# Gate stage of a graph and expert network: one activation per hidden chunk, its two parts made on VectorE, turned parts evicted by ScalarE, router sums two steps later

## What is computed

```python
x = x + gnn(layernorm(x), src, dst, edge_weight, ...)        # x: 12500 x 256
xf = layernorm(x)
H = gelu(xf @ W1 + b1)                                        # 1024 hidden values per token
probs = softmax(H @ Wg + bg)                                  # 8 experts
assign = argmax(probs)
y = H @ Wd[assign] + bd[assign]
x = x + probs[assign] * y
```

## Time and profile before

| what | us |
|---|---|
| median of 3 runs | 3556.47 (3550.64 to 3558.81) |
| the profiled execution | 3553.28 |
| its span on the core | 3551.5 |
| TensorE matmul busy / VectorE busy / ScalarE busy in the span | 2995.6 / 2470.9 / 1287.2 |
| first matmul of the gate stage's products to the last | 2443.3 to 3075.1 |

### The profile page before, as it was taken

One profiled execution on the slowest core, in us unless ns is written; L12 is line 12 of the kernel. 1 busy time (PEld: TensorE's weight loads), 2 busy tenths in 40 slices (PEclk: granted clock), 3 DMA queues, 4 the chain that ended last, 5 costly groups with the idle time before them and its releaser, 6 DMA issues. The chain is left out here.

```text
span 3551.5 us, 67236 instructions
## 1 busy us (share of the span) xinstructions
PE 2995.6 (84%) x20000; PEld 2455.1 (69%) x20001; DVE 2470.9 (70%) x6086; ACT 1287.2 (36%) x2250; POOL 722.6 (20%) x706
## 2 busy tenths in 40 slices
PE   4776668888888886999999999996888888669998
PEld 2333347777777776888888888444666667469998
DVE  8999557777777774666666666335787777576665
ACT  3111346666666662000000000363545545353332
POOL 1000005555655552000000000000212121212222
PEclk9888559999999998999999999998999999879999
DMA  4221017777777777998999887001334333366664
GB/s 122 81 73 44 1 37 290 282 285 293 294 284 278 287 278 269 318 315 317 316 314 316 316 315 267 6 0 36 138 125 161 137 149 133 122 229 208 211 211 146
DMA packets 214801, 710.45 MB, mean 200 GB/s; under 512 B 28495, under 2 KB 104313, under 8 KB 189514
## 3 DMA queue, kind: packets, MB, share of 16 engines
q1 hardware_dynamic: 130778, 405.55, 34.8%
q0 software_dynamic: 83952, 304.02, 21.8%
HBM read 383.91 MB, written 340.05 MB: 204 GB/s over the span
## 5 line engine op out<-in xcount | busy, mean ns | idle before, releaser
L1232 PE MATMUL coll_ps_sum<-coll_rows,coll_hot 128*128 128x256 f32 x3724 | 822.5, 380 | 19.0 <-DVE coll_hot L1174 18.9
L1232 PEld LDWEIGHTS coll_ps_sum<-coll_rows,coll_hot 128*128 128x128 f32 x3724 | 701.4, 190 | 111.3 <-DVE coll_hot L1174 19.1
L1174 DVE TENSOR_SCALAR coll_hot<-coll_nodes,coll_rows 128x128 f32<-128x128 f32 x1862 | 495.0, 342 | 281.4 <-PE coll_ps_sum L1232 259.6
L927 PE MATMUL send_ps_msg<-send_parts,send_pick 128*128 128x256 f32 x3584 | 547.0, 302 | 25.9 <-ACT send_msg L960 23.6
L801 POOL DMA_INDIRECT messages<-send_msg,send_to x448 | 477.5, 1066 | 383.6 <-ACT send_msg L960 232.7
L960 ACT ACTIVATE send_msg<-send_ps_msg 128x1024 f32<-128x1024 f32 x448 | 456.8, 1026 | 262.5 <-PE send_ps_msg L927 200.0
L927 PEld LDWEIGHTS send_ps_msg<-send_parts,send_pick 128*128 128x128 f32 x3584 | 480.0, 201 | 33.5 <-ACT send_msg L960 26.0
L844 DVE TENSOR_SCALAR send_pick<-send_ps_local,edges_down 128x1024 fp32r<-128x1024 f32 x224 | 287.5, 1284 | 178.3 <-PE send_ps_local L914 86.3
L1265 ACT ACTIVATE nodes_hid<-coll_ps_turned 128x256 f32 (+1 forms) x98 | 37.6, 383 | 810.0 <-PE coll_ps_turned L1078 810.0
L2148 PE MATMUL exp_ps_y<-exp_w_hi,exp_hT_hi 128*128 x840 | 247.0, 294 | 0.9 <-DVE exp_hT_lo L2100 0.9
L1647 ACT ACTIVATE gate_act_h<-gate_ps_h,gate_b_sb 128x512 f32<-128x512 f32 x200 | 137.2, 686 | 294.4 <-PE gate_ps_h L1875 293.3
(11 more groups left out here) (302 smaller groups left out, 5148.4 us busy)
## 6 DMA issues: line engine op xcount, KB each, us to landing
coll_rows<-messages SPq DMA_DIRECT2D x98, 1300.0 KB, 6.7
coll_rows<-messages SPq DMA_DIRECT2D x98, 1170.0 KB, 6.9
exp_pay<-regions SPq DMA_DIRECT2D x105, 646.0 KB
send_window<-node_rows SPq DMA_DIRECT2D x112, 128.0 KB
node_rows<-sort_xn SPq DMA_DIRECT2D x25, 512.0 KB, 5.1
coll_own<-node_rows SPq DMA_DIRECT2D x98, 128.0 KB, 4.3
sort_xt<-in_x_dram SPq DMA_DIRECT2D x24, 512.0 KB, 4.4
gate_xt<-in_x_dram SPq DMA_DIRECT2D x24, 384.0 KB
```

The source lines that it names most:

```text
L927: ins = pe.matmul(ps_msg[:, q % 2, a, :], pick[:, q * RUN + a, :], parts[:, s % 2, part, :], start=(part == 0), stop=(part == 1))
L1174: ins = dve.tensor_scalar(hot[:, j, :], nodes[:], rows[:, s, j, ROW_ID:ROW_ID + 1], rows[:, s, j, ROW_W:ROW_W + 1], ALU.is_equal, ALU.mult)
L1232: ins = pe.matmul(ps_sum[:, s, 0:D], hot[:, j, :], rows[:, s, j, 0:D], start=(j == 0), stop=(j == CJ - 1))
```

## The change

ScalarE applies Gelu once per step, into `act_h`. VectorE rounds `act_h` to `act_hi` with a copy, waits for it, and subtracts. `keep_back` moves from VectorE to ScalarE, behind the Gelu of its step. TensorE adds a step's logits two steps later instead of one, between the two halves of a product; those of step 7 stay where they were, those of step 6 go into the next chunk's first product. GpSimd waits for the payload's evictions itself before it sends.

```diff
@@ -1588,6 +1588,7 @@
                 def send(i, s):
                     pool.wait_ge(where_ready, i + 1)
                     pool.wait_ge(x2_copied, i + 1)
+                    pool.wait_ge(back_ready, KC * (i + 1))
                     pool.sem_inc(pool_turn, 1)
                     for j in range(CH):
                         pool.indirect_dma_start(
@@ -1630,6 +1631,15 @@
                     act.activation(xnT_hi[:, s], ps_x[:].rearrange("p c f -> p (c f)").rearrange("p (k n) -> p k n", k=DH),
                                    ACT.Copy).then_inc(xnT_hi_ready, 1)
 
+                def keep_back(i, s, k, before):
+
+                    if k == 0 and later(i, 2):
+
+                        act.wait_ge(sent[s], 16 * CH * before)
+                    act.wait_ge(back_done, KC * i + k + 1)
+                    act.sem_inc(act_turn, 1)
+                    act.activation(pay[:, s, :, k * P:(k + 1) * P], ps_b[:, k % 2, :, :], ACT.Copy).then_inc(back_ready, 1)
+
                 def keep_logits(i):
                     act.wait_ge(logit_sum, i + 1)
                     if later(i):
@@ -1644,8 +1654,11 @@
                         act.wait_ge(h_done, KC * i + k + 1)
 
                         act.sem_inc(act_turn, 1)
-                        act.activation(act_h[:, k % 2, :], ps_h[:, k % 2, :], ACT.Gelu, bias=b_sb[:, k:k + 1])
-                        act.activation(act_hi[:, k % 2, :], ps_h[:, k % 2, :], ACT.Gelu, bias=b_sb[:, k:k + 1]).then_inc(h_ready, 1)
+                        act.activation(act_h[:, k % 2, :], ps_h[:, k % 2, :], ACT.Gelu, bias=b_sb[:, k:k + 1]).then_inc(h_ready, 1)
+                        if k > 0:
+                            keep_back(i, s, k - 1, before)
+                        elif later(i):
+                            keep_back(i - 1, 1 - s, KC - 1, None)
                         if k == 0 and later(i):
                             keep_logits(i - 1)
                         if k == XN_AT and not is_last(i):
@@ -1654,6 +1667,7 @@
                 second_output(0)
                 keep_xnT(0, 0)
                 all_chunks(act, chunk)
+                keep_back(LAST, 0, KC - 1, None)
                 keep_logits(LAST)
 
             @block.vector
@@ -1711,16 +1725,9 @@
 
                     dve.wait_ge(h_ready, KC * i + k + 1)
                     dve.sem_inc(dve_turn, 1)
+                    steps.link(dve.tensor_copy(act_hi[:, k % 2, :], act_h[:, k % 2, :]))
                     dve.tensor_tensor(act_lo[:, k % 2, :], act_h[:, k % 2, :], act_hi[:, k % 2, :].bitcast(F32),
                                       ALU.subtract).then_inc(act_lo_ready, 1)
-
-                def keep_back(i, s, k, before):
-
-                    if k == 0 and later(i, 2):
-
-                        dve.wait_ge(sent[s], 16 * CH * before)
-                    dve.wait_ge(back_done, KC * i + k + 1)
-                    dve.tensor_copy(pay[:, s, :, k * P:(k + 1) * P], ps_b[:, k % 2, :, :]).then_inc(back_ready, 1)
 
                 def choose(i, s):
 
@@ -1760,10 +1767,6 @@
                 def chunk(i, s, before):
                     steps.restart()
                     for k in range(KC):
-                        if k > 0:
-                            keep_back(i, s, k - 1, before)
-                        elif later(i):
-                            keep_back(i - 1, 1 - s, KC - 1, None)
                         keep_rest(i, k)
                         if not is_last(i):
                             if k == RESIDUAL_AT:
@@ -1787,7 +1790,6 @@
                 keep_xnT_rest(0, 0)
                 all_chunks(dve, chunk)
                 steps.restart()
-                keep_back(LAST, 0, KC - 1, None)
                 choose(LAST, 0)
                 find_places(LAST, 0)
 
@@ -1871,6 +1873,10 @@
                             pe.wait_ge(h_ready, KC * i + k - 1)
 
                         for q in range(DH):
+                            if q > 0 and k >= 2:
+                                add_logits(i, k - 2)
+                            elif q > 0 and k == 0 and later(i):
+                                add_logits(i - 1, KC - 2)
                             for w, a in ((w_hi, xnT_hi), (w_hi, xnT_lo), (w_lo, xnT_hi)):
                                 ins = pe.matmul(ps_h[:, k % 2, :], w[:, q, k * P:(k + 1) * P], a[:, s, q, :],
                                                 start=(q == 0 and w is w_hi and a is xnT_hi),
@@ -1886,9 +1892,7 @@
                             count(i - 1)
                         if k == XN_AT and not is_last(i):
                             turn_xn(i + 1)
-                        if k > 0:
-                            add_logits(i, k - 1)
-                        elif later(i):
+                        if k == 0 and later(i):
                             add_logits(i - 1, KC - 1)
                         if k == 0 and not is_last(i):
                             turn_back(i + 1)
@@ -1897,6 +1901,7 @@
                 turn_xn(0)
                 all_chunks(pe, chunk)
                 back(LAST, KC - 1)
+                add_logits(LAST, KC - 2)
                 add_logits(LAST, KC - 1)
                 turn_logits(LAST)
                 count(LAST)
```

## The result

The changed kernel took 3574.27 us (median of 7 runs, 3553.29 to 3578.45), the kernel before 3556.03 (7 runs): ratio 1.0049, 95% interval 1.003 to 1.0068. The forecast was 3543.3 with a range to 3562, so both the direction and the range were missed.

What follows compares the result with a forecast made beforehand. The prediction took the loop of TensorE, Gelu and VectorE's chain to the normalisation as the bound. 24 x 0.42 plus 3.1 from the clock gave 13.2 us less, 3556.47 to 3543.3, range 3532 to 3562.

Steps and rivals of the forecast that it cites:

- What bounds the kernel: Gate stage: the loop of TensorE, Gelu and VectorE's chain of some 10 us to the normalisation sets the chunk's period.
- Rival B: Gate stage: TensorE becomes the bound, 25 x 2.46 = 60 us less, 3496; chance 0.04.
- The activation and the copy: Step 2: second activation goes, VectorE's copy with link takes 0.46, so the moments start 0.12 us earlier.
- the bounds 0.35 and 0.73: VectorE's copy with link: lower and upper limits around 0.46, for a loop gain of 0.75 or -0.39 us.
- T0: End of the product of step 0 on TensorE's timeline of a full-clock chunk, 2725.41 in the profile before.
- The eviction goes, the copy with its link comes: 0.61 - 0.46 = 0.15 gained in each: VectorE at steps 3 and 4: replacing the eviction by the copy gains 0.15 us in each step.
- The 0.12 of step 2: VectorE at step 2: moments start at 2734.15 and not 2734.27, 0.12 us gained.
- I take it that the falls go, and all of the 3.1 is gained: TensorE's clock: waits of 1.6 and 1.7 bring no falls, saving 0.26 us a chunk, 12 times: 3.1.
- Rival A: TensorE's clock falls behind the second wait in 12 of 24 chunks: 17.9 less 13.2, 4.7 us slower, 3561; chance 0.16.
- a gain of 13.2: Whole gate stage: 24 chunks x 0.42 plus 3.1 from the clock, 13.2 us gained in all.
- The eviction on ScalarE: ScalarE, in the second activation's slot of 0.68: costs nothing, with bounds of 0.57 to 0.69 for its length.
- rival C: Loop shortened less, by bubbles of 0.1 in five places of the loop or falls that stay: 3550 to 3560; chance 0.20.

Runs made afterwards that it cites:

- the last experiment: Changed kernel with the gap before step 3's copy closed, find_places moved behind the normalisation, and GpSimd's x-row copy put before its sends: ratio to the kernel before 0.9887.
- both gaps closed: Changed kernel with VectorE's wait for Gelu and its increment issued before waiting for its last small operation, at steps 3 and 4: ratio to the kernel before 0.9956.
- logits alone: Kernel before with only the logits moved two steps later, inside the next product: ratio to the kernel before 1.0010.
- gap of step 4 closed: Changed kernel with the wait for Gelu and its increment issued early at step 4 only: ratio to the kernel before 0.9975.

## Why the prediction was wrong

**What bounds the kernel** was right: VectorE's row from the moments to the normalisation sets the chunk (closing its gaps shortened the chunk by 0.37, and taking the places out of it by another 1.2 once nothing else was late), the wait for `act_lo` is split and not removed (1.62 and 1.88, forecast 1.6 and 1.7), and the last experiment gains what the shorter row promises. Rival B fell with it.

**The activation and the copy** were right in size: copy 0.43, subtraction 0.46 behind it, as forecast; the bounds 0.35 and 0.73 were not needed. The product of step 2 ended 6.63 after T0 and not 6.54, but T0 came 7.36 behind `turn_xn` and not 7.45 (2705.61 to 2712.97), so TensorE's part of the loop is the 13.99 of the forecast.

**"The eviction goes, the copy with its link comes: 0.61 - 0.46 = 0.15 gained in each"** is the first step that failed. I compared lengths, and took it that the copy would start where the eviction had started. The eviction had been the cover of the wait and increment of `keep_rest`; without it they stood bare, 0.18 at step 3 and 0.18 at step 4 by the kernel with both gaps closed, 0.37 of its interval. The 0.12 of step 2 came, and as much was lost behind it: from the moments to the normalisation 7.95 (2721.79 to 2729.74; 7.82 before, 7.52 forecast), and from the product of step 2 to `turn_xn` 11.56 (2719.60 to 2731.16), where it was 11.57 before (2731.95 to 2743.52) and 11.15 was forecast. So the loop gained nothing. At full clock the interval even went from 25.47 to 25.56, which goes with the delay of the logits, for logits alone has 25.58 with the old row; it is as short as the average before, 25.59 (2472.05 to 3035.03 in 22 intervals), only because the old falls were gone. The prediction itself named gaps in VectorE's chain as a sign that it would be wrong.

**"I take it that the falls go, and all of the 3.1 is gained"** is the second, and the dear one. It rested on a second wait of 1.7, which the gap at step 4 made 1.88. At 1.7 there are indeed no falls (both gaps closed, gap of step 4 closed); at 1.88 there were nine, and they cost 1.6 each, since no wait follows. So the second error came out of the first. Rival A described what happened and its price was near, 1.49 against 1.6, but it had a chance of 0.16. Its sum was made with a gain of 13.2 that was not there: with nearly no gain (22 x 0.03 = 0.7), nine falls of 1.6 are 14.4 - 0.7 = 13.7 slower, against 12.5 measured; the two intervals at the start of the stage gained the 1.1 between them.

**The eviction on ScalarE** cost nothing, as forecast: 0.59, in the slot of the second activation.

```profile
L1641 ACT ACTIVATE gate_pay<-gate_ps_b 128x512 f32<-128x512 f32 x200 | 118.2, 591 | 0.6 <-PE gate_ps_b L1828 0.3
```

**Bubbles inside products**, rival C, are not there: three matmuls, two for the logits and three more took 0.23 each. **GpSimd's new wait** cost nothing: its sends still wait for the places alone, 508.2 us in 25 times and 502.3 before.

The Trainium skill says that a semaphore costs nothing extra between chained VectorE operations (VectorE: DVE Perf Modes, § The DRAIN you can't avoid). Here that holds nearly: the subtraction starts 0.03 behind the end of the copy that it is linked to. But a second wait, on a computed value and with an increment behind it, cost 0.18 more where no long operation ran beside it.

## What to carry to other kernels

Ask of an instruction that is taken away what ran beside it: the sequencer's own work (computing a wait's value, waiting, incrementing) was hidden behind an eviction of 0.69 and cost 0.18 behind an operation of 0.16, and it could be hidden again by putting it between that operation and the wait for it. If a wait of TensorE is split, look at what follows the last part: a fall of the clock that another wait swallows cost 0.2 to 0.3 here, the same fall at the end of the loop 1.6. And moving work off the row that bounds the kernel is worth its whole length only if the queue that it feeds, here GpSimd's sends, is not late next, and if no other engine's copy comes to lie beside an operation on which something waits.

## What was not expected of the hardware

The step from no falls to many is narrow: waits of 1.82 before `turn_xn` with one of 1.68 ahead brought none, 1.88 with 1.62 or 1.4 ahead brought 9 to 12 in 22 chunks, 2.17 brought 21. One wait of 2.46, with a short one behind it, brought only 11 (the kernel before), one of 2.7 brought 13.

GpSimd's copy between two SBUF tiles (1.06) stretches VectorE's operations on SBUF that lie beside it: a subtraction of two SBUF tiles took 2.07 in place of 0.69, more than the whole length of the copy. The Trainium skill says that GpSimd's SBUF interfaces are shared with VectorE and contend with its instructions of two SBUF inputs (GPSIMD Engine Reference, § Specifications); the trace agrees, and gives the price, 1.38 in each of 23 chunks. With the copy moved, the subtraction of step 5 met it (1.41) in one chunk and the rounding copy of that step (1.29) in the next, and TensorE waited for neither. The same happens unseen in the changed kernel, where it meets the rounding copy of step 6: 1.05 in place of 0.43.
